# Gathering each tile of routed tokens by a slot-to-token table, in place of a scatter into a cleared buffer

## The chip, the cores and the metric

One core of a Trainium2 chip runs the kernel. The metric is the device time of one execution in microseconds (us). PE is TensorE, DVE is VectorE, ACT is ScalarE, POOL is GpSimd and SP is SyncE; SP and POOL issue the DMA transfers here.

## The reference

Four residual blocks run over x of shape (4, 512, 512), that is 2,048 tokens of 512 numbers, each behind a layer norm: a matmul with fp8-rounded operands, a mixture-of-experts FFN, cross attention with 16 heads, and a gated FFN with a Hadamard transform. Only the second matters here:

```python
xt = x.reshape(B * S, H)
sh_mid = gelu(einsum('th,ehd->ted', xt, Wsh_up))          # 2 shared experts, D = 256
shared_out = einsum('ted,edh->th', sh_mid, Wsh_down)
probs = softmax(xt @ W_router)                            # 16 routed experts
top_v, top_i = top_k(probs, 2)
gate = sum(one_hot(top_i, 16) * top_v[..., None], axis=1)
rt_mid = gelu(einsum('th,ehd->ted', xt, Wrt_up))
routed_out = einsum('ted,edh->th', rt_mid * gate[:, :, None], Wrt_down)
```

## The kernel before

The kernel runs phase by phase. `experts_phase` does the FFN with experts, from about 135 to 490 us of the span. Every float32 product is made in three passes from operands split into a high part (by ACT, `*_hi`) and a rest (by DVE, `*_lo`).

**Routing.** DVE writes the normalised tokens to `xn` (16 tiles of 128 tokens), PE transposes them (`turn_all`) and multiplies them by the router's weights (`route`). DVE then picks two experts for each token (`choose`). PE counts, by products with a triangle and with ones, how many tokens ahead of each one chose the same expert (`place_tokens`). From that DVE works out a slot for each token and choice, `slot[0]` and `slot[1]`, and the expert of each tile of 128 slots, `tile_expert`. Each expert's slots begin on a tile of their own, so there are up to NSLOT = 47 tiles.

**Dense part.** Eight units (four batches of 512 tokens, two shared experts) run on PE as `up(s)` and `down(s)`: `up` gives two banks, ACT puts the gelu on them and splits them, DVE makes the rest (`low(s)`), `down` gives four tiles, and DVE adds each to `x_res` (`add(s)`). `down` has three banks in turn, so that its tile n waits for the addition of tile n - 3. For batches 2 and 3 the transposed tokens are made again in the midst of the units (`turn_again` on PE, `again_hi` on ACT, `again_lo` on DVE). On each engine the order is written out by hand; PE's is up(0), up(1), place_tokens, down(0), up(2), turn_again(2), up(3), a wait for again_lo(2), down(1), down(2), turn_again(3), up(4), and so on. DVE's is assign_places, assign_slots(0), add(0), assign_slots(1), assign_tiles, low(2), again_lo(2), add(1), low(3), add(2), again_lo(3), and so on.

**The way of the tokens.** POOL sets a row of zeros, SP writes it over all of the DRAM tensor `tokens_by_expert` (47 tiles, `cleared`), and then POOL scatters each tile of `xn` to the slots of its first and of its second choice, 32 indirect DMAs (`scattered`). SP has one queue in order: for tile i it loads the expert's up weights and down weights (512 KB each, ring of four), then tile i of the tokens into `xg` (256 KB, ring of three, and for i = 0 only when all scatters have landed), then it stores the output of tile i - 6.

**Routed stage.** For each of the 47 tiles PE transposes `xg` (`turn(n)`, line 1153), multiplies by the up weights, transposes the gelu'd middle and multiplies by the down weights; ACT and DVE split all operands, ACT writes the output `y_out`. The attention phase then gathers the two outputs of each token from DRAM by `slot` with indirect DMAs on POOL (lines 1448 and 1455).

Of the kernel before, what the change touches and what calls it, by code (L numbers as in the profile page):

```python
# [5 lines left out]
F32 = mybir.dt.float32  # L6
F32R = mybir.dt.float32r
BF16 = mybir.dt.bfloat16
U32 = mybir.dt.uint32
# [553 lines left out]
def experts_phase(nc, Wsh_up, Wsh_down, Wrt_up, Wrt_down, W_router, x_res, ident, stats, head_weights,  # L563
# [4 lines left out]

    xg_dram = nc.dram_tensor("tokens_by_expert", (NSLOT * P, D), F32, kind="Internal").ap()
    with ExitStack() as ctx:  # L572
        al = Alloc(nc, ctx, "e")
        up_raw = al.sb("up_raw", [2, KD, DE])
# [3 lines left out]
        down_hi = al.sb("down_hi", [2, KE, D], F32R)  # L578
        down_lo = al.sb("down_lo", [2, KE, D], F32R)
        router_raw = al.sb("router_raw", [KD, E_RT])  # L580
        zeros = al.sb("zeros", [KD])
        probs = al.sb("probs", [NT, E_RT])
        rest = al.sb("rest", [NT, E_RT])
        first = al.sb("first", [NT, E_RT])
# [14 lines left out]
        passed = al.sb("passed", [NSLOT, E_RT])  # L599
        tile_f = al.sb("tile_f", [NSLOT])  # L600
        tile_expert = al.sb("tile_expert", [NSLOT], I32)
        xn = al.sb("xn", [NT, D])
        xg = al.sb("xg", [XG_RING, D])
        bank = [al.ps(f"bank{i}", [S]) for i in range(8)]
# [1 line left out]
        down_bank = bank[4:7]  # L606
        aux = bank[7]
        turn_bank = bank[0:7]
        logits_bank = aux[:, 0:NT * E_RT].rearrange("p (t e) -> p t e", e=E_RT)
        place_bank = aux[:, 0:(NT + 1) * E_RT].rearrange("p (t e) -> p t e", e=E_RT)  # L610
        xgT_bank, mid_bank = bank[0:2], bank[2:4]
# [34 lines left out]
        gate_chain = al.sem("gate_chain")  # L646
        shifted = al.sem("shifted")
        const_ready = al.sem("const_ready")
        zeros_ready = al.sem("zeros_ready")
        cleared = al.sem("cleared")  # L650
        chosen_ready = al.sem("chosen_ready")
        placed = al.sem("placed")
        slots_ready = al.sem("slots_ready")
        map_ready = al.sem("map_ready")
        scattered = al.sem("scattered")
        up_done = al.sem("up_done")
        gelu_ready = al.sem("gelu_ready")
        mid_hi_ready = al.sem("mid_hi_ready")
# [19 lines left out]
        @block.sync  # L678
        def _(sp):
            sp.dma_start(router_raw[:, :, :], rows(W_router)).then_inc(router_in, 16)  # L680
            for i in range(E_SH):
                sp.dma_start(up_raw[:, i], rows(Wsh_up[i])).then_inc(up_in[i], 16)
                sp.dma_start(down_raw[:, i], rows(Wsh_down[i])).then_inc(down_in[i], 16)
            sp.wait_ge(zeros_ready, 2)
            sp.dma_start(xg_dram.rearrange("(t p) d -> p t d", p=P),
                         xg[:, 0:1, :].to_broadcast([P, NSLOT, D])).then_inc(cleared, 16)

            up_flat = Wrt_up.rearrange("e (k p) m -> e p k m", p=P)
            down_flat = Wrt_down.rearrange("e (k p) m -> e p k m", p=P)

            def load(i):
                r = i % RAW_RING
                expert = sp.value_load(tile_expert[0:1, i:i + 1], min_val=0, max_val=E_RT - 1)
                if i < E_SH:
                    sp.wait_ge(up_ready, i + 1)
                elif i < RAW_RING:
                    sp.wait_ge(up_done, UNITS * KE)
                else:
                    sp.wait_ge(up_ready, E_SH + i - RAW_RING + 1)
                sp.dma_start(up_raws[r], up_flat[bass.ds(expert, 1)]).then_inc(up_in[r], 16)  # L700
                if i < E_SH:
                    sp.wait_ge(down_ready, i + 1)
                elif i >= RAW_RING:
                    sp.wait_ge(down_ready, E_SH + i - RAW_RING + 1)
                sp.dma_start(down_raws[r], down_flat[bass.ds(expert, 1)]).then_inc(down_in[r], 16)
                if i >= XG_RING:
                    sp.wait_ge(xg_turned, i - XG_RING + 1)
                if i == 0:
                    sp.wait_ge(scattered, 16 * 2 * NT)
                sp.dma_start(xg[:, i % XG_RING, :], xg_dram[i * P:(i + 1) * P, :]).then_inc(xg_in[i % XG_RING], 16)  # L710

            def store(i):
                sp.wait_ge(y_ready, i + 1)
                sp.dma_start(y_dram[i * P:(i + 1) * P, :], y_out[:, i % Y_RING, :]).then_inc(y_stored[i % Y_RING], 16)

            sp.wait_ge(map_ready, 1)
            for i in range(NSLOT):
                load(i)
                if i >= STORE_LAG:
                    store(i - STORE_LAG)  # L720
            for i in range(NSLOT - STORE_LAG, NSLOT):
                store(i)
            for i in range(Y_RING):
                sp.wait_ge(y_stored[i], 16 * len(range(i, NSLOT, Y_RING)))

        @block.gpsimd
        def _(pool):
            nc.clear_and_free_semaphores(retired)
            pool.memset(zeros[:, :], 0.0).then_inc(zeros_ready, 1)
            pool.memset(xg[:, 0, :], 0.0).then_inc(zeros_ready, 1)  # L730
            pool.wait_ge(zeros_ready, 1)
            for e in range(E_RT):
                pool.memset(rank[:, :, e:e + 1], float(E_RT - e)).then_inc(const_ready, 1)
            pool.memset(ones[:, :], 1.0).then_inc(const_ready, 1)
            pool.memset(chosen[:, NT, :], 0.0).then_inc(const_ready, 1)
            for i in range(2):
                pool.memset(run[i][:, 0:8], 0.0).then_inc(const_ready, 1)
            pool.iota(tile_no[:, :], [[1, NSLOT]], base=0, channel_multiplier=0,
                      allow_small_or_imprecise_dtypes=True).then_inc(const_ready, 1)
            pool.wait_ge(const_ready, E_RT + 5)  # L740
            pool.affine_select(below[:, :], ones[:, :], [[1, P]], ALU.is_gt, 0.0, base=0,
                               channel_multiplier=-1).then_inc(const_ready, 1)

            for name in "qkvo":
                head_weights.load(pool, name, 0)
            pool.wait_ge(cleared, 16)
            for i in range(2):
                pool.wait_ge(slots_ready, i + 1)
                for j in range(NT):
                    pool.indirect_dma_start(  # L750
                        xg_dram[:, :], bass.IndirectOffsetOnAxis(ap=slot[i][:, j:j + 1], axis=0), xn[:, j, :], None,
                        bounds_check=NSLOT * P - 1, oob_is_err=False).then_inc(scattered, 16)
        @block.scalar
        def _(act):
            def unit(s):
# [124 lines left out]
        def _(dve):  # L880
# [35 lines left out]
            def choose():  # L916
                dve.wait_ge(exp_ready, 1)
                link(dve.tensor_reduce(top[:, :], probs[:, :, :], AX.X, ALU.add))
                link(dve.reciprocal(inv[:, :], top[:, :]))
                link(dve.tensor_tensor(probs[:, :, :], probs[:, :, :], wide(inv), ALU.mult))  # L920
                dve.wait_ge(const_ready, E_RT + 6)
                pick(probs[:, :, :], first[:, :, :], gate[0])
                link(dve.scalar_tensor_tensor(out=rest[:, :, :], in0=first[:, :, :], scalar=-2.0, in1=probs[:, :, :],
                                              op0=ALU.mult, op1=ALU.add))
                pick(rest[:, :, :], rest[:, :, :], gate[1])
                dve.tensor_tensor(chosen[:, 0:NT, :], first[:, :, :], rest[:, :, :], ALU.add).then_inc(chosen_ready, 1)
# [21 lines left out]
            def assign_tiles():  # L948
                link(dve.tensor_tensor(passed[0:1], tile_no[0:1, :].unsqueeze(2).to_broadcast([1, NSLOT, E_RT]),
                                       run[0][0:1, 8:].unsqueeze(1).to_broadcast([1, NSLOT, E_RT]), ALU.is_ge))  # L950
                link(dve.tensor_reduce(tile_f[0:1, :], passed[0:1], AX.X, ALU.add))
                dve.tensor_scalar(tile_expert[0:1, :], tile_f[0:1, :], float(E_RT - 1), None,
                                  ALU.min).then_inc(map_ready, 1)

            def norm(b):
                for i in range(TB * b, TB * (b + 1)):
# [41 lines left out]
            assign_tiles()  # L998
            low(2)
            again_lo(2)  # L1000
            add(1)
            low(3)
            add(2)
            again_lo(3)
            low(4)
            add(3)
# [40 lines left out]

        @block.tensor
        def _(pe):
            def turn_all(b):  # L1050
                for j in range(TB):
                    n = TB * b + j
                    pe.wait_ge(xn_ready, n + 1)
                    if n >= 7:
                        pe.wait_ge(x32_ready, n - 6)
                    for k in range(KD):
                        ins = pe.transpose(turn_bank[n % 7][:, k * P:(k + 1) * P], xn[:, n, k * P:(k + 1) * P], ident[:, :])
                    ins.then_inc(x32_turned, 1)
# [71 lines left out]
            up(3)  # L1130
            pe.wait_ge(again_ready, TB)
            down(1)
            down(2)
            turn_again(3)
            up(4)
            pe.wait_ge(again_ready, 2 * TB)
# [31 lines left out]
            def turn_mid(n):  # L1168
                pe.wait_ge(gmid_ready, n + 1)
                if n == 0:  # L1170
                    pe.wait_ge(slots_ready, 2)
                elif n == 1:
                    pe.wait_ge(added, UNITS * TB)
                else:
# [978 lines left out]
```

## Time and profile before

| | |
|---|---|
| median of 3 runs | 2151.6 us (2144.74 to 2157.84) |
| the profiled execution | 2148.4 us, its span 2146.8 us |
| PE busy | 2007.4 us, 94% of the span |
| DVE busy | 1318.8 us, 61% |
| ACT busy | 842.2 us, 39% |
| POOL busy | 863.7 us, 40% |
| mean of TensorE's granted clock | 0.978 of full speed |

The span runs from the first to the last instruction of one profiled execution. A share of busy time is a mean over stages; what a change in one stage is worth has to be read in that stage. In a timeline a row gives the start, the length, the engine and line, and in brackets how long the engine had stood idle before and what ended it. "issue" is a wait that the profile can't put down to anything, "remote" an event from outside the engines.

### The profile page before, as it was taken

How to read it: one execution, taken by the hardware profiler on the slowest of the kernel's cores; microseconds unless marked ns; L12 is line 12 of the kernel's file. 1: busy time of each engine (PE TensorE's matmuls, PEld its weight loads, DVE VectorE, ACT ScalarE, POOL GpSimd, SP SyncE). 2: the span in 40 equal slices, each digit the busy share in tenths (PEclk: the TensorE clock that was granted, in tenths of full speed). 3: DMA queues.
4: the chain of work that ended last, by engine and by line, in shares of the span. 5: the costliest groups of instructions: out<-in, count | busy, mean ns of one | idle time of the engine just before them, and what ended most of it. 6: DMA issues, size and time to landing. Idle time of an engine off the chain costs nothing. (4 is left out here: it accounts for less than half of the span.)

```text
span 2146.8 us, 29048 instructions
## 1 busy us (share of the span) xinstructions
PE 2007.4 (94%) x9845; PEld 1663.7 (77%) x9849; DVE 1318.8 (61%) x2072; ACT 842.2 (39%) x1639; POOL 863.7 (40%) x739
## 2 busy tenths in 40 slices
PE   4987799994899999999999999999989999999999
PEld 4776577773778888888788888888867888888887
DVE  8975368887677766768676566666675333333333
ACT  4532158882434444445444444444432111111111
POOL 1104100003677766666766657665551222202200
PEclk9988899997999999999999999999999999999999
DMA  8366259994566656566555555555530011001002
GB/s 287 121 235 257 74 187 388 394 352 149 177 187 187 181 170 186 164 187 182 167 152 159 166 156 156 154 161 165 158 113 30 30 30 30 20 10 29 0 1 78
DMA packets 170320, 323.70 MB, mean 151 GB/s; under 512 B 16113, under 2 KB 41585, under 8 KB 170225
## 3 DMA queue, kind: packets, MB, share of 16 engines
q1 hardware_dynamic: 155120, 272.12, 40.8%
q0 software_dynamic: 15104, 50.34, 7.2%
q8 instruction: 55, 0.90, 0.2%
q14 instruction: 41, 0.33, 0.0%
HBM read 210.73 MB, written 111.67 MB: 150 GB/s over the span
## 5 line engine op out<-in xcount | busy, mean ns | idle before, releaser
L1393 POOL TENSOR_TENSOR t_pT_lo<-t_pT_raw,t_pT_hi 128x512 fp32r<-128x512 f32 x256 | 328.3, 1302 | 215.2 <-ACT t_pT_hi L1509 213.5
L1617 DVE TENSOR_REDUCE t_sums<-t_score 128x1 f32<-128x512 f32 x256 | 169.5, 688 | 130.3 <-PE t_score L52 129.9
L1991 DVE TENSOR_TENSOR f_lin<-f_lin,f_silu 128x512 f32<-128x512 f32 x64 | 44.8, 700 | 290.6 <-PE f_lin L52 290.6
L1524 ACT ACTIVATE t_probs<-t_score,t_sums 128x512 f32<-128x512 f32 x256 | 175.0, 684 | 84.3 <-DVE t_sums L1617 69.0
L1607 DVE STREAM_TRANSPOSE t_blocks<-t_probs 128x512 f32<-128x512 f32 x256 | 172.6, 693 | 20.4 <-ACT t_probs L1524 20.1
L1599 DVE SCALAR_TENSOR_TENSOR x_res<-t_out,t_sums,x_res 128x512 f32<-128x512 f32 x256 | 179.4, 741 | 4.7 <-PE t_out L52 4.5
L1509 ACT ACTIVATE t_pT_hi<-t_pT_raw 128x512 fp32r<-128x512 f32 x256 | 159.9, 625 | 1.1 <-DMA t_pT_raw<-turned_blocks 1.1
L1952 ACT ACTIVATE f_silu<-f_gate 128x512 f32<-128x512 f32 x64 | 38.3, 598 | 299.1 <-PE f_gate L52 299.1
L1503 ACT ACTIVATE t_o_hi<-t_o 128x512 fp32r<-128x512 f32 x64 | 38.3, 598 | 218.0 <-PE t_o L52 218.0
L1489 ACT ACTIVATE t_k_hi<-t_score 128x512 fp32r<-128x512 f32 x64 | 38.3, 598 | 204.6 <-PE t_score L52 200.9
L52 PE MATMUL t_score<-t_wv_hi,t_cT_hi 128*128 128x256 f32 x416 | 117.9, 283 | 0.7 <-ACT t_probs L1524 0.7
L52 PE MATMUL t_score<-t_wv_lo,t_cT_hi 128*128 128x256 f32 x416 | 117.9, 283 | 0.0
L52 PE MATMUL t_score<-t_wv_hi,t_cT_lo 128*128 128x256 f32 x416 | 117.8, 283 | 0.0
L52 PE MATMUL t_out<-t_wo_hi,t_o_hi 128*128 128x512 f32 x256 | 105.0, 410 | 12.8 <-DVE t_o_lo L1592 8.1
L2012 DVE TENSOR_TENSOR x_res<-f_down,x_res 128x512 f32<-128x512 f32 x128 | 88.1, 689 | 44.1 <-PE f_down L52 44.1
L52 PE MATMUL t_score<-t_k_hi,t_q_hi 128*128 128x512 f32 x256 | 102.8, 402 | 12.8 <-DVE t_v_lo L1586 4.8
L1582 DVE TENSOR_TENSOR t_k_lo<-t_score,t_k_hi 128x512 fp32r<-128x512 f32 x64 | 44.3, 691 | 113.2 <-ACT t_k_hi L1489 109.2
L52 PE MATMUL t_score<-t_cT_hi,t_wk_hi 128*128 128x512 f32 x256 | 101.5, 397 | 12.2 <-DVE t_cT_lo L1681 12.2
L1455 POOL DMA_INDIRECT t_blocks<-outputs_by_expert,slot x4 | 4.6, 1143 | 268.9 <-POOLq L572 267.9
L52 PE MATMUL t_q<-t_xT_hi,t_wq_hi 128*128 128x512 f32 x256 | 100.5, 393 | 2.8 <-DVE t_xT_lo L234 2.8
L52 PE MATMUL t_score<-t_k_lo,t_q_hi 128*128 128x512 f32 x256 | 101.3, 396 | 0.0
L52 PE MATMUL t_out<-t_wo_lo,t_o_hi 128*128 128x512 f32 x256 | 101.3, 396 | 0.0
(325 smaller groups left out, 6004.3 us busy)
## 6 DMA issues: line engine op xcount, KB each, us to landing
turned_blocks<-t_blocks SPq DMA_DIRECT2D x256, 256.0 KB
t_pT_raw<-turned_blocks SPq DMA_DIRECT2D x256, 256.0 KB, 4.1
e_up_raw<-in_L_ffn_Wrt_up_dram SPq DMA_DIRECT2D x47, 512.0 KB, 6.4
e_down_raw<-in_L_ffn_Wrt_down_dram SPq DMA_DIRECT2D x47, 512.0 KB, 5.9
tokens_by_expert<-e_xg SPq DMA_DIRECT2D x1, 12032.0 KB, 41.4
e_xg<-tokens_by_expert SPq DMA_DIRECT2D x47, 256.0 KB, 6.1
outputs_by_expert<-e_y_out SPq DMA_DIRECT2D x47, 256.0 KB, 6.2
wq_raw<-in_L_xattn_Wq_dram POOLq DMA_DIRECT2D x32, 256.0 KB, 4.6
```

The lines of the kernel that those rows point to most:

```text
L52: ins = pe.matmul(out, w(k), x(k), start=(k == 0 and j == 0), stop=(k == k_tiles - 1 and j == 2))
L1393: pool.tensor_tensor(pT_lo[:, q], pT_raw[:, q], f32(pT_hi[:, q]), ALU.subtract).then_inc(p_ready, 1)
L1489: act.activation(k_hi[:, :], score_bank[0][:, :], ACT.Copy).then_inc(k_hi_ready, 1)
L1503: act.activation(o_hi[:, :].rearrange("p (u q j) -> p q u j", q=Q4, j=BLK), o_bank[:, :].rearrange("p (q u j) -> p q u j", q=Q4, j=BLK), A ...
L1509: act.activation(pT_hi[:, q], pT_raw[:, q], ACT.Copy).then_inc(p_hi_ready, 1)
L1524: act.activation(probs[:, t % 2, :], score_bank[t][:, :], ACT.Exp, bias=neg_max[:, t:t + 1], accum_out=inv[:, p, t:t + 1]).then_inc(exp_re ...
L1582: dve.tensor_tensor(k_lo[:, :], score_bank[0][:, :], f32(k_hi[:, :]), ALU.subtract).then_inc(k_ready, 1)
L1599: dve.scalar_tensor_tensor(out=x_tile, in0=out_bank[t % 2][:, :], scalar=inv[:, p, t:t + 1], in1=x_tile, op0=ALU.mult, op1=ALU.add).then_i ...
L1607: dve.transpose(blocks[:, :, :, t, :].rearrange("p a t j -> p t a j"), probs[:, t % 2, :].rearrange("p (t a j) -> p t a j", a=Q4, j=BLK)). ...
L1617: dve.tensor_reduce(neg_max[:, t:t + 1], score_bank[t][:, :], AX.X, ALU.max, negate=True).then_inc(max_ready, 1)
L1991: dve.tensor_tensor(lin_bank[k][:, :], lin_bank[k][:, :], silu[:, k, :], ALU.mult).then_inc(mid_done, 1)
L2012: dve.tensor_tensor(x_tile, down_bank[t][:, :], x_tile, ALU.add).then_inc(added, 1)
```

## The change

The place of the routed tokens in DRAM, its clearing and the scatters go. In their stead SP stores `xn` as it is to DRAM (`normalised_tokens`, four transfers of 1 MB, each when its batch is normalised). A table is made that says for each slot which token is in it: a slot is split into its place in a tile (low seven bits) and its tile. DVE makes two one-hots, `at_place` (128 places for each of 16 token tiles) and `at_tile` (47 tiles, once weighted by the token's row and once by its tile number), in `mark(i)` for choice i. PE multiplies them, 16 products of 94 columns for each choice, all into one bank (`find_tokens(i)`), and DVE puts row and tile number together (`number_tokens`). POOL then gathers tile n of the tokens by column n of that table, straight from DRAM into `xg`. Empty slots have token 0. SP's loop is left with the weights and the stores. The new steps stand at fixed places of the orders written by hand.

```diff
@@ SP
-            sp.wait_ge(zeros_ready, 2)
-            sp.dma_start(xg_dram.rearrange("(t p) d -> p t d", p=P),
-                         xg[:, 0:1, :].to_broadcast([P, NSLOT, D])).then_inc(cleared, 16)
+            for b in range(B):
+                sp.wait_ge(xn_ready, TB * (b + 1))
+                sp.dma_start(xn_dram[b * S:(b + 1) * S, :].rearrange("(t p) d -> p t d", p=P),
+                             xn[:, TB * b:TB * (b + 1), :]).then_inc(xn_stored, 16)
...
-                if i >= XG_RING:
-                    sp.wait_ge(xg_turned, i - XG_RING + 1)
-                if i == 0:
-                    sp.wait_ge(scattered, 16 * 2 * NT)
-                sp.dma_start(xg[:, i % XG_RING, :], xg_dram[i * P:(i + 1) * P, :]).then_inc(xg_in[i % XG_RING], 16)
@@ POOL
-            pool.memset(zeros[:, :], 0.0).then_inc(zeros_ready, 1)
-            pool.memset(xg[:, 0, :], 0.0).then_inc(zeros_ready, 1)
-            pool.wait_ge(zeros_ready, 1)
...
-            pool.wait_ge(cleared, 16)
-            for i in range(2):
-                pool.wait_ge(slots_ready, i + 1)
-                for j in range(NT):
-                    pool.indirect_dma_start(
-                        xg_dram[:, :], bass.IndirectOffsetOnAxis(ap=slot[i][:, j:j + 1], axis=0), xn[:, j, :], None,
-                        bounds_check=NSLOT * P - 1, oob_is_err=False).then_inc(scattered, 16)
+            pool.wait_ge(xn_stored, 16 * B)
+            pool.wait_ge(tokens_ready, 1)
+            for n in range(NSLOT):
+                if n >= XG_RING:
+                    pool.wait_ge(xg_turned, n - XG_RING + 1)
+                pool.indirect_dma_start(
+                    xg[:, n % XG_RING, :], None, xn_dram[:, :], bass.IndirectOffsetOnAxis(ap=token[:, n:n + 1], axis=0),
+                    bounds_check=NT * P - 1, oob_is_err=False).then_inc(xg_in[n % XG_RING], 16)
@@ DVE
+            def mark(i):
+                if i == 1:
+                    dve.wait_ge(token_found, 1)
+                link(dve.tensor_scalar(place_u[:, :], slot[i][:, :], P - 1, None, ALU.bitwise_and))
+                link(dve.tensor_scalar(tile_u[:, :], slot[i][:, :], 7, None, ALU.logical_shift_right))
+                link(dve.tensor_copy(place_of[:, :], place_u[:, :]))
+                link(dve.tensor_copy(tile_of[:, :], tile_u[:, :]))
+                each = lambda a, n: a.unsqueeze(1).to_broadcast([P, NT, n])
+                of = lambda a, n: a.unsqueeze(2).to_broadcast([P, NT, n])
+                link(dve.tensor_tensor(at_place[:, :, :], each(place_no[:, :], P), of(place_of[:, :], P), ALU.is_equal))
+                link(dve.tensor_tensor(at_tile[:, :, 0, :], each(tile_no[:, :], NSLOT), of(tile_of[:, :], NSLOT),
+                                       ALU.is_equal))
+                link(dve.tensor_tensor(at_tile[:, :, 1, :], at_tile[:, :, 0, :], of(tile_count[:, :], NSLOT), ALU.mult))
+                dve.tensor_scalar(at_tile[:, :, 0, :], at_tile[:, :, 0, :], row_no[:, 0:1], None,
+                                  ALU.mult).then_inc(marked, 1)
+
+            def number_tokens():
+                dve.wait_ge(token_found, 2)
+                link(dve.tensor_copy(tile_f[:, :], token_bank[:, 0:NSLOT]))
+                dve.scalar_tensor_tensor(out=token[:, :], in0=token_bank[:, NSLOT:2 * NSLOT], scalar=float(P),
+                                         in1=tile_f[:, :], op0=ALU.mult, op1=ALU.add).then_inc(tokens_ready, 1)
...
             again_lo(2)
+            mark(0)
             add(1)
             low(3)
+            mark(1)
             add(2)
+            number_tokens()
             again_lo(3)
@@ PE
+            def find_tokens(i):
+                pe.wait_ge(marked, i + 1)
+                for j in range(NT):
+                    ins = pe.matmul(token_bank, at_place[:, j, :], at_tile[:, j, :, :].rearrange("p a n -> p (a n)"),
+                                    start=(i == 0 and j == 0), stop=(i == 1 and j == NT - 1))
+                ins.then_inc(token_found, 1)
...
             down(1)
+            find_tokens(0)
             down(2)
+            find_tokens(1)
             turn_again(3)
...
                 if n == 0:
-                    pe.wait_ge(slots_ready, 2)
+                    pe.wait_ge(tokens_ready, 1)
```

Three short `iota` instructions on POOL (the numbers 0 to 127, the row, and 0 to 15) take the place of its two `memset`s.

## Rows read from the trace of the kernel before

**Rows 1.** Windows: us, PE, PEld, DVE, ACT, POOL busy, PEclk, DMA share, GB/s.

```profile
150.00:160.00 10.00, 10.00 (x69) 10.00 (x69) 0.00 (x0) 4.28 (x6) 0.00 (x0) 0.72 1.05 410
200.00:230.00 30.00, 9.09 (x18) 5.24 (x18) 1.72 (x3) 1.65 (x3) 19.14 (x20) 0.59 0.49 191
260.00:270.00 10.00, 10.00 (x45) 8.05 (x44) 3.36 (x5) 1.98 (x4) 0.00 (x0) 1.00 0.00 1
500.00:508.00 8.00, 8.00 (x33) 6.84 (x34) 5.63 (x8) 0.60 (x1) 6.17 (x7) 0.62 0.92 319
320.00:400.00 80.00, 75.20 (x478) 62.19 (x477) 69.04 (x81) 70.26 (x120) 0.00 (x0) 1.00 1.06 390
```

**Rows 2.** Instructions of line 750, the scatters: ns least/median/most, first and last start.

```profile
L750 POOL DMA_INDIRECT tokens_by_expert<-e_xn,slot x32: 976/976/1106, 184.0 to 223.9; - x32
```

**Rows 3.** Timeline of ACT beside the scatters.

```profile
206.27 0.60 ACT L783 ACTIVATE e_xT_hi<-e_bank 128x512 fp32r<-128x512 f32 x1 [5.75 <-remote]
229.46 0.58 ACT L759 ACTIVATE e_bank<-e_bank 128x512 f32<-128x512 f32 x1 [22.59 <-remote]
```

**Rows 4.** Timeline of PE, 177 to 242.

```profile
177.56 1.12 PE L1111 MATMUL e_bank<-e_chosen,e_ones 128*128 128x256 bf16 x16
...
193.76 0.66 PE L1077 MATMUL e_bank<-ident,e_xn 128*128 128x128 f32 x4 [1.31 <-DVE e_xT_lo L968]
...
199.60 0.40 PE L52 MATMUL e_bank<-e_xT_hi,e_up_lo 128*128 128x512 f32 x1
207.65 0.79 PE L52 MATMUL e_bank<-e_down_hi,e_mid_hi 128*128 128x512 f32 x1 [7.65 <-issue]
...
214.00 0.39 PE L52 MATMUL e_bank<-e_down_lo,e_mid_hi 128*128 128x512 f32 x1 [1.50 <-issue]
...
239.75 0.39 PE L52 MATMUL e_bank<-e_down_lo,e_mid_hi 128*128 128x512 f32 x1
239.98 0.40 PE L52 MATMUL e_bank<-e_down_hi,e_mid_lo 128*128 128x512 f32 x1
241.16 1.53 PE L1077 MATMUL e_bank<-ident,e_xn 128*128 128x128 f32 x12 [0.79 <-DVE x_res L902]
```

**Rows 5.** Instructions of line 1153, the transpositions of the 47 routed tiles.

```profile
L1153 PE MATMUL e_bank<-ident,e_xg x188: 270/273/331, 294.2 to 477.4; 128*128 128x128 f32 x188
```

**Rows 6.** Waits, 320 to 470: us in all, times, longest.

```profile
PEld e_bank L1153 <- DMA e_xg<-tokens_by_expert: 25.2, 37, 1.3
ACT e_y_out L861 <- DMA outputs_by_expert<-e_y_out: 20.1, 38, 1.7
```

**Rows 7.** DMA issues of the page, the clearing: KB, us to landing.

```profile
tokens_by_expert<-e_xg SPq DMA_DIRECT2D x1, 12032.0 KB, 41.4
```

**Rows 8.** Timeline of DVE, operations of the sizes that the change adds.

```profile
167.39 2.29 DVE L962 TENSOR_TENSOR e_xT_lo<-e_x,e_xT_hi 128x2048 fp32r<-128x2048 f32 x1
...
180.51 0.81 DVE L936 TENSOR_TENSOR e_run<-e_run 128x16 f32<-128x16 f32 x4
...
187.29 0.93 DVE L949 TENSOR_TENSOR e_passed<-e_tile_no,e_run 1x752 f32<-1x752 f32 x1
```

**Rows 9.** Timelines of POOL, ACT and PE beside eight gathers.

```profile
543.67 1.07 POOL L1448 DMA_INDIRECT ffn_raw<-outputs_by_expert,slot  x1 [25.10 <-DVE t_cT_lo L1681]
...
550.28 0.39 PE L52 MATMUL t_score<-t_cT_hi,t_wk_lo 128*128 128x512 f32 x1
...
552.36 0.60 ACT L1489 ACTIVATE t_k_hi<-t_score 128x512 fp32r<-128x512 f32 x1 [3.73 <-remote]
...
553.78 0.69 PE L52 MATMUL t_score<-t_k_hi,t_q_hi 128*128 128x512 f32 x1 [3.11 <-issue]
554.26 0.63 PE L52 MATMUL t_score<-t_k_lo,t_q_hi 128*128 128x512 f32 x1
```

**Rows 10.** Instructions of line 1455, gathers of the outputs, and their landing.

```profile
L1455 POOL DMA_INDIRECT t_pT_raw<-outputs_by_expert,slot x4: 1014/1271/1653, 494.7 to 503.8; - x4
...
DMA to landing us min/median/max: 4.1/4.7/5.3
```

More of the change, by code:

```diff
@@ L564, in experts_phase @@
                   y_dram, gate, slot, retired):
-    xg_dram = nc.dram_tensor("tokens_by_expert", (NSLOT * P, D), F32, kind="Internal").ap()
+    xn_dram = nc.dram_tensor("normalised_tokens", (NT * P, D), F32, kind="Internal").ap()
     with ExitStack() as ctx:
@@ L580, in experts_phase @@
         router_raw = al.sb("router_raw", [KD, E_RT])
-        zeros = al.sb("zeros", [KD])
         probs = al.sb("probs", [NT, E_RT])
@@ L601, in experts_phase @@
         tile_expert = al.sb("tile_expert", [NSLOT], I32)
+        place_no, row_no, tile_count = al.sb("place_no", [P]), al.sb("row_no", [1]), al.sb("tile_count", [NT])
+        place_u, tile_u = al.sb("place_u", [NT], U32), al.sb("tile_u", [NT], U32)
+        place_of, tile_of = al.sb("place_of", [NT]), al.sb("tile_of", [NT])
+        at_place = al.sb("at_place", [NT, P], BF16)
+        at_tile = al.sb("at_tile", [NT, 2, NSLOT], BF16)
+        token = al.sb("token", [NSLOT], U32)
         xn = al.sb("xn", [NT, D])
@@ L608, in experts_phase @@
         turn_bank = bank[0:7]
+        token_bank = aux[:, (NT + 1) * E_RT:(NT + 1) * E_RT + 2 * NSLOT]
         logits_bank = aux[:, 0:NT * E_RT].rearrange("p (t e) -> p t e", e=E_RT)
@@ L648, in experts_phase @@
         const_ready = al.sem("const_ready")
-        zeros_ready = al.sem("zeros_ready")
-        cleared = al.sem("cleared")
+        xn_stored = al.sem("xn_stored")
+        marked, token_found, tokens_ready = al.sem("marked"), al.sem("token_found"), al.sem("tokens_ready")
         chosen_ready = al.sem("chosen_ready")
@@ L654, in experts_phase @@
         map_ready = al.sem("map_ready")
-        scattered = al.sem("scattered")
         up_done = al.sem("up_done")
@@ L739, in _ @@
                       allow_small_or_imprecise_dtypes=True).then_inc(const_ready, 1)
-            pool.wait_ge(const_ready, E_RT + 5)
+            pool.iota(place_no[:, :], [[1, P]], base=0, channel_multiplier=0,
+                      allow_small_or_imprecise_dtypes=True).then_inc(const_ready, 1)
+            pool.iota(row_no[:, :], [[1, 1]], base=0, channel_multiplier=1,
+                      allow_small_or_imprecise_dtypes=True).then_inc(const_ready, 1)
+            pool.iota(tile_count[:, :], [[1, NT]], base=0, channel_multiplier=0,
+                      allow_small_or_imprecise_dtypes=True).then_inc(const_ready, 1)
+            pool.wait_ge(const_ready, E_RT + 8)
             pool.affine_select(below[:, :], ones[:, :], [[1, P]], ALU.is_gt, 0.0, base=0,
@@ L920, in choose @@
                 link(dve.tensor_tensor(probs[:, :, :], probs[:, :, :], wide(inv), ALU.mult))
-                dve.wait_ge(const_ready, E_RT + 6)
+                dve.wait_ge(const_ready, E_RT + 9)
                 pick(probs[:, :, :], first[:, :, :], gate[0])
```

## The prediction

> **What bounds the kernel now.** I read the page first. TensorE (PE) is busy for 94% of the span, as the table above says, so what a change is worth depends on the few places where PE stands still. I then cut the experts phase into windows and looked for a low PE figure. The dense part has PE at 10.00 us of 10, but from 200 to 230 PE is busy for 9.09 us of 30, and DVE and ACT for 1.7 us each [rows 1]. The DMA engines moved 191 GB/s there, where the clearing transfer reached 410. So all engines wait, and not for bandwidth.
>
> The instructions of POOL and the timelines of ACT and PE say more. POOL issues the 32 scatters from 184.0 to 223.9, one every 1.29 us [rows 2]. ACT splits its last transposed tile at 206.27, though PE had started that transposition at 193.76 and ended it by 194.4, and then does nothing for 22.59 us [rows 3, 4]. PE waits for this chain until 207.65. Then come matmuls inside one product, which wait for no semaphore, and one of them stands behind 1.50 us of "issue" [rows 4]. The pace is normal again soon after the last scatter. I read this as: while scatters are in flight, the sequencers hand out instructions very slowly. How that comes about no row shows.
>
> In the routed stage each of the 47 tiles takes (477.4 - 294.2) / 46 = 3.98 us [rows 5]. The DMA share is 1.06 at 390 GB/s; over 150 us and some 37 tiles PE's weight loads wait 25.2 us for `e_xg` and ACT 20.1 us for the stores [rows 1, 6]. That is a loop near the limit of the DMA engines, with ACT and DVE busy for 70.26 and 69.04 us of 80.
>
> **The change, part by part.**
>
> *Clearing and scatter out.* The clearing (12,032 KB, 41.4 us to land [rows 7]) lies under work of PE that needs none of it, so it is worth nothing by itself. The four 1 MB stores of `xn` in its place are a third of the bytes and hidden in the same stretch. With the scatters goes, if I read it rightly, the stall. What is that worth? up(3) ends at 199.85. down(1) and down(2) are 24 matmuls each at 0.23 us (the spacing of the two before turn_again) = 5.6 us each, then comes the 0.8 us wait for add(2): turn_again(3) could start at 199.85 + 11.2 + 0.8 = 211.85. It started at 241.16 [rows 4]. **Gross: -29.3 us.**
>
> *mark(0) and mark(1) on DVE, find_tokens on PE.* A mark has four operations on 16 elements at 0.2 us (0.84 with their gaps), one on 2,048 elements, as `e_xT_lo` (2.29), three on 752, as `e_passed` (2.79), and four gaps of 0.04: 6.1 us [rows 8]. Place decides what shows of it, so I went through both orders. again_lo(2) ends at 195.7 (0.6 us on PE, ACT and DVE each behind 193.76). mark(0) runs 195.7 to 201.8. down(1) runs 199.85 to 205.45 and its tiles are added from 202.7 to 206.2: no wait. find_tokens(0) is 16 short bf16 products; the 16 of place_tokens, 136 columns wide in the mean against 94, took 1.12 us [rows 4]: until 206.55. mid_hi(3) needs down(1)'s end, its second half comes at 207.4, low(3) ends at 208.1, and mark(1), behind it, at 214.2. Behind mark(1) stands add(2). down(2) does three tiles until 210.75; its fourth needs add(2)'s first addition, 214.2 + 0.7 = 214.9. **That is a new stall of PE of 4.1 us.** The fourth tile ends at 216.3, find_tokens(1) at 217.4, and it covers the old 0.8 us wait. turn_again(3) starts at 217.4, so the additions cost 217.4 - 211.85 = 5.6 us. Bounds: 2.2 us (the products alone, marks hidden) and 14.4 us (marks and products fully exposed).
>
> *Clock.* After an idle of 3.11 us PE came back at the lower of its two levels, 1.2 GHz: matmuls of 0.69 and 0.63 us where 0.39 is usual, for some 3 us, eight matmuls each 0.2 us late = 1.6 us [rows 9]. I add 1.6 for the new stall (bounds 0 and 3.2): turn_again(3) at 219.0. **So far: 219.0 - 241.16 = -22.2 us.** All that follows in the dense part hangs on a PE at 10 of 10 us and moves up with it. number_tokens is two small operations beside transpositions.
>
> *Gathers.* 47 indirect gathers on POOL replace 47 plain loads on SP. The first three are issued near 219, some 50 us before they are needed. A later one waits for turn(n - 3), so it has 3 x 3.98 = 12 us; gathers took 1.0 to 1.65 us on POOL and landed 4.1 to 5.3 us behind their issue [rows 10]: on time. Bytes stay 1.5 MiB a tile. On SP's queue each load and store has one transfer fewer ahead, so the waits for `e_xg` and for stores shrink, but by the DMA engines at most 183 x (1 - 390/410) = 8.9 us can be had. Against that stands that gathers disturb engines too: eight were issued from 543.67 on, and beside them ACT took `t_k_hi` at 552.36, though PE had ended its input at 550.7; 1.7 us late, 0.21 us a gather [rows 9]. Over 47 tiles that is 10 us if nothing absorbs it, but ACT has 20.1 / 37 = 0.5 us of idle a tile. I take 0 for the loop, with -8.9 and +10 as ends.
>
> The Trainium skill, "SBUF — State Buffer", section "SBUF: two separate sides", speaks against this part: GpSimd and a VectorE operation in a two-port mode exclude each other for the whole instruction, so that descriptors of a GpSimd DMA can't be written meanwhile. The trace agrees at most in part: one gather took 1.65 us where most of its neighbours took 1.0. By the rule alone the time would be that of the second rival, 2151; by the row it is the sum below.
>
> **Sum.** -29.3 + 5.6 + 1.6 + 0 = -22.2 us by the clock times above. The profiled execution took 2148.4 us (span 2146.8), the median of the runs is 2151.6: profiling adds nothing that can be seen, so the stall belongs to the ordinary run as well. 2151.6 - 22.2 = **2129.4 us**. A difference under 0.5%, 10.8 us, can hardly be told from none.
>
> **The rivals.**
>
> 1. *Each gather holds up the sequencers.* In the scatters' stall single instructions lost 1.50 us [rows 4]. If each gather costs the loop half of one such hold, 0.75 us, the stage gains 47 x 0.75 = 35 us: 2151.6 - 22.2 + 35 = 2164, slower. It turns the sign from 22.2 / 47 = 0.47 us a tile. For it: [rows 9] show a delay of 0.21 us a gather. Against it: from 500 to 508, in the midst of sixteen gathers, PE was busy for 8.00 us of 8 [rows 1], and one gather in 4 us is a third of that density. 9%.
> 2. *Gathers wait for DVE.* DVE is busy 69.04 / 80 x 3.98 = 3.43 us a tile [rows 1]. If a gather of 1.0 us fits only beside that, the period is 4.43 us, +0.45 x 47 = +21: 2151, no change. Against it: the longest gather beside DVE's work took 1.65 us [rows 10]. 8%.
> 3. *The stall isn't the scatters'.* Something else holds the engines from 200 to 229 and stays; the marks vanish in it and only the products, 2.2 us, are added: 2154, no change. Against it: the stall begins some 10 us behind the first scatter and ends with them. 7%. By the skill's same section transfers and engines have separate ports, so scatters shouldn't slow an engine; no row shows ports.
> 4. *The loop gains as well.* With `xg` off SP's queue the period falls to the DMA engines' limit: 2129.4 - 8.9 = 2120.5. 18%.
>
> My own case, the loop within 5 us of today's, has 58%.
>
> **How the numbers follow.** Faster by over 0.5% (below 2140.8): my case and rival 4, less 0.02 for costs near their upper bounds, 0.74. Within 0.5%: rivals 2 and 3 and that rest, 0.18 with a little of rival 1. Slower: the rest of rival 1, 0.08. The range starts at 2117, rival 4 with marks of 4 instead of 6.1 us; it reaches to 2150, which is where the upper bounds together lead (-29.3 + 14.4 + 3.2 + 10 = -1.7), and leaves out half of the no-change cases and the slower one. The likeliest case alone: 2122 to 2137.
>
> **What would show it.** Windows behind 195 have PE at 9 to 10 of 10 us but for one idle of about 4 us ahead of the fourth tile of down(2), ended by DVE's `x_res`. Each mark is 6 us of DVE. PE's first transposition of `e_xg` starts near 272 instead of 294.2. From there on a tile takes 3.9 to 4.1 us, with one gather each on POOL, and PE's wait for `e_xg` falls or moves to the weights. I am wrong if "issue" or "remote" idles stand on PE and ACT all through the routed stage (rival 1), if gathers last 2 us and more and PE waits for them (rival 2), or if the stall near 200 is still there (rival 3).

## The result, and the profile after

The changed kernel took 2133.42 us in the median of 4 runs (2123.97 to 2140.55), the kernel before 2152.72 us (2144.74 to 2157.84). The ratio on record is 0.9901 with a 95% interval of 0.9874 to 0.9928, so the gain lies between 15.5 and 27.1 us: faster, by about 1%. The two medians by themselves differ by 19.3 us. The profiled execution took 2140.55 us (span 2138.9), which is at the slow end of its four runs. Why it is there matters for reading it, so I begin with the stages, worked out as differences of start times in the two timelines of PE:

| stretch | before | after | difference |
|---|---|---|---|
| first transposition of `xn` to up(0) | 28.14 | 37.75 | +9.6 |
| up(0) to turn_again(3) | 77.04 | 53.81 | -23.2 |
| turn_again(3) to the first transposition of `e_xg` | 53.0 | 52.8 | -0.2 |
| first to last transposition of `e_xg` | 183.2 | 189.0 | +5.8 |
| from there to the first product of attention | 22.5 | 20.7 | -1.7 |
| attention and FFN | 1646.8 | 1647.7 | +0.9 |

With 1.0 us that the phase began later this makes -7.8, the difference of the spans (-7.9) but for rounding. Windows of the changed kernel (columns as in [rows 1]):

```profile
150.00:160.00 10.00, 10.00 (x50) 10.00 (x49) 0.61 (x1) 2.26 (x5) 0.00 (x0) 0.50 0.86 335
160.00:180.00 20.00, 20.00 (x83) 18.87 (x82) 5.01 (x5) 7.92 (x9) 0.00 (x0) 0.50 0.00 1
200.00:230.00 30.00, 25.03 (x140) 19.88 (x139) 21.56 (x36) 6.53 (x13) 0.00 (x0) 0.94 0.22 71
```

Between 200 and 230 PE is busy for 25.03 us where it was 9.09 [rows 1]: the stall is gone. But from 150 to 180 the granted clock is at the lower level, 1.2 GHz, where the window of before showed 0.72. PE does the same routing work without a pause in both, so it takes longer. It isn't part of the change, as the experiments show: the same kernel has either length. What decides between them no run shows. Now the place where the prediction had put a new wait, first on PE and then on DVE:

```profile
216.06 0.87 PE L1087 MATMUL e_bank<-e_at_tile,e_at_place 128*128 128x94 bf16 x16
...
224.86 0.79 PE L52 MATMUL e_bank<-e_down_hi,e_mid_hi 128*128 128x512 f32 x1 [3.66 <-DVE x_res L910]
225.45 0.63 PE L52 MATMUL e_bank<-e_down_lo,e_mid_hi 128*128 128x512 f32 x1
...
227.59 1.09 PE L1087 MATMUL e_bank<-e_at_tile,e_at_place 128*128 128x94 bf16 x16
228.57 1.53 PE L1118 MATMUL e_bank<-ident,e_xn 128*128 128x128 f32 x12
```

```profile
219.50 2.29 DVE L973 TENSOR_TENSOR e_at_place<-e_place_no,e_place_of 128x2048 bf16<-128x2048 f32 x1
221.83 0.94 DVE L974 TENSOR_TENSOR e_at_tile<-e_tile_no,e_tile_of 128x752 bf16<-128x752 f32 x1
222.81 0.94 DVE L976 TENSOR_TENSOR e_at_tile<-e_at_tile,e_tile_count 128x752 bf16<-128x752 bf16 x1
223.78 0.42 DVE L977 TENSOR_SCALAR e_at_tile<-e_at_tile,e_row_no 128x752 bf16<-128x752 bf16 x1
224.12 1.88 DVE L910 TENSOR_TENSOR x_res<-e_bank,x_res 128x512 f32<-128x512 f32 x3
```

The addition at 224.12 comes behind mark(1), PE's fourth tile of down(2) behind that addition, after 3.66 us of idle, and its six matmuls run at the lower clock (0.79 and 0.63 us). In the routed stage (transpositions, gathers with ns least/median/most, and waits from 320 to 470; they answer to [rows 5, 6]):

```profile
L1196 PE MATMUL e_bank<-ident,e_xg x188: 270/272/417, 281.4 to 470.4; 128*128 128x128 f32 x188
```

```profile
L757 POOL DMA_INDIRECT e_xg<-normalised_tokens,e_token x47: 997/1300/1518, 230.1 to 456.6; - x47
```

```profile
POOL e_xg L757 <- PE e_bank L1196: 96.9, 34, 3.7
ACT e_y_out L869 <- DMA outputs_by_expert<-e_y_out: 23.0, 33, 2.8
...
PEld e_bank L52 <- issue: 13.3, 31, 2.5
```

No row has PE waiting for `e_xg` any more, and POOL waits for PE instead, 2.8 us each time. ACT still waits for the stores, 23.0 us in 33 waits where it was 20.1 in 38 [rows 6].

### The profile page after: what moved, and what is told of

Its sections match the earlier page's. It is cut to its first block and busy times, and to the rows that moved or that the text cites. A ratio compares the mean times of both kernels' runs of the same rounds, so it can differ in the third digit from the quotient of the medians.

```text
span 2138.9 us, 29117 instructions
## 1 busy us (share of the span) xinstructions
PE 2019.6 (94%) x9877; PEld 1675.9 (78%) x9881; DVE 1329.2 (62%) x2090; ACT 843.0 (39%) x1639; POOL 890.9 (42%) x755
## 5 line engine op out<-in xcount | busy, mean ns | idle before, releaser
L757 POOL DMA_INDIRECT e_xg<-normalised_tokens,e_token x47 | 59.7, 1270 | 256.1 <-PE e_bank L1196 167.2
L52 PE MATMUL t_out<-t_wo_hi,t_o_lo 128*128 128x512 f32 x256 | 102.5, 400 | 0.0
```

The costliest lines, as they stand in the source:

```text
L52: ins = pe.matmul(out, w(k), x(k), start=(k == 0 and j == 0), stop=(k == k_tiles - 1 and j == 2))
L757: pool.indirect_dma_start(xg[:, n % XG_RING, :], None, xn_dram[:, :], bass.IndirectOffsetOnAxis(ap=token[:, n:n + 1], axis=0), bounds_chec ...
```

## The experiments

All times are medians of the runs. The ratio is to the kernel before, run beside on the same chip; where there is none, the kernel ran once. e1, e8, e9, e3 and e4 leave routed tokens out or fetch others; they are tests, and their time is no offer.

| kernel | us | ratio, 95% interval | first transposition to up(0) | up(0) to turn_again(3) | routed stage |
|---|---|---|---|---|---|
| before | 2152.72 | | 28.14 | 77.04 | 183.2 |
| after | 2133.42 | 0.9901 (0.9874 to 0.9928) | 37.75 | 53.81 | 189.0 |
| e12, after again | 2127.52 | one run | 28.36 | 52.69 | 186.6 |
| e1, no scatters | 2129.0 | 0.9874 (0.9836 to 0.9911) | 37.53 | 48.06 | 188.5 |
| e8, 16 scatters | 2134.3 | 0.9905 (0.9877 to 0.9932) | 28.15 | 52.19 | 181.8 |
| e9, 32 gathers instead | 2160.82 | one run | 37.55 | 76.45 | 184.6 |
| e10, scatters held apart | 2129.07 | one run | 37.54 | 47.91 | 181.5 |
| e2, clearing back | 2133.71 | 0.9891 (0.9844 to 0.9937) | 37.62 | 54.07 | 185.3 |
| e3, plain loads | 2137.3 | 0.9918 (0.9889 to 0.9947) | 37.75 | 53.87 | 186.2 |
| e4, rows in order | 2128.44 | 0.9883 (0.9843 to 0.9923) | 28.35 | 53.73 | 181.5 |
| e5, mark(1) later | 2130.8 | 0.9884 (0.9857 to 0.9911) | 28.36 | 48.49 | 187.8 |
| e6, empty slots skipped | 2119.75 | 0.9843 (0.9812 to 0.9873) | 32.28 | 53.36 | 179.1 |
| e7, e5 and e6 | 2116.74 | 0.9821 (0.9795 to 0.9846) | 29.06 | 48.49 | 178.1 |
| e11, e7 and four outputs | 2113.62 | 0.9819 (0.9790 to 0.9849) | 38.45 | 48.50 | 173.2 |

The last three columns come from each kernel's one profile. The first of them is near 28 or near 38 (32 once) whatever the kernel, so it is to be left out when kernels are compared.

### Is it the scatters? (e1, e8)

```diff
# e1, on the kernel before
-            for i in range(2):
-                pool.wait_ge(slots_ready, i + 1)
-                for j in range(NT):
-                    pool.indirect_dma_start(xg_dram[:, :], ..., xn[:, j, :], ...).then_inc(scattered, 16)
...
-                    sp.wait_ge(scattered, 16 * 2 * NT)
+                    sp.wait_ge(cleared, 16)
# e8, on the kernel before
-            for i in range(2):
+            for i in range(1):
...
-                    sp.wait_ge(scattered, 16 * 2 * NT)
+                    sp.wait_ge(scattered, 16 * NT)
```

> The kernel before, with its 32 scatters left out; SP's first load of a token tile waits for the clearing instead, so that all routed tiles are zeros and the routed output is wrong. If the scatters cause the stall of 200 to 230 us (my theory), PE has no idle 'issue' rows there, turn_again(3) starts about 47 to 48 us behind up(0) instead of 77.0, and the time is 29 us below the kernel before, near 2123. If something else holds the engines there (rival: fetching of instructions, or what the early part of the dense stage does by itself), the 77 us and the time stay.

> The kernel before with the 16 scatters of the first choice alone; half of the routed tokens are left zero, so the output is wrong. The scatters last 20.6 us instead of 41.3. If the engines are held whenever scatters are in flight, the stall lasts half as long or less: the loss against no scatters falls from 29 to between 5 and 12 us (it began some 10 us behind the first scatter). If the loss doesn't depend on the number of scatters, it stays at 29.

Without scatters the dense stretch takes 48.06 us instead of 77.04: the 32 scatters cost 29.0 us. With 16 of them it takes 52.19: 4.1 us, less than the 5 to 12 expected. The cost isn't proportional: the second half of the scatters does 25 of the 29 us.

### Scatters, or any indirect transfers of POOL, and in what manner? (e9, e10)

```diff
# e9, on the kernel before: 32 gathers at the scatters' place, eight buffers
                 for j in range(NT):
+                    n = NT * i + j
+                    if n >= 8:
+                        pool.wait_ge(burst[n % 8], 16 * (n // 8))
                     pool.indirect_dma_start(
-                        xg_dram[:, :], ..., xn[:, j, :], ...).then_inc(scattered, 16)
+                        spare[:, n % 8, :], None, xg_dram[:, :],
+                        bass.IndirectOffsetOnAxis(ap=slot[i][:, j:j + 1], axis=0),
+                        bounds_check=NSLOT * P - 1, oob_is_err=False).then_inc(burst[n % 8], 16)
# e10, on the kernel before
                 for j in range(NT):
+                    if NT * i + j >= 2:
+                        pool.wait_ge(scattered[j % 2], 16 * ((NT * i + j) // 2))
                     pool.indirect_dma_start(
...
```

> The kernel before with each of its 32 scatters replaced at its place by a gather of the same number of rows, from the cleared DRAM tensor by the same indices into eight spare buffers (at most eight in flight); the routed tokens are left zero, so the output is wrong. Is it the scatter or any burst of indirect transfers from POOL that holds the engines? If only scatters do (writes to DRAM), turn_again(3) starts 48 to 50 us behind up(0), as without scatters. If any burst does, it starts at about 77, as before.

> The kernel before with its 32 scatters held apart: POOL issues one only when the last but one has landed, so two are in flight at most; the output is the reference's. If the engines are held because scatters pile up (many in flight), they are held little or not at all: turn_again(3) starts 48 to 55 us behind up(0) instead of 77.0, though the scatters last longer. If each scatter in flight holds them, the loss is as long as the scatters last, and it starts at 77 or later.

With 32 gathers the stretch takes 76.45 us, as with the scatters. Timeline of PE, beside POOL's row for those gathers:

```profile
220.78 0.58 PE L52 MATMUL e_bank<-e_down_hi,e_mid_lo 128*128 128x512 f32 x1 [2.10 <-issue]
241.40 0.80 PE L52 MATMUL e_bank<-e_down_hi,e_mid_hi 128*128 128x512 f32 x1 [20.04 <-DVE x_res L908]
```

```profile
L755 POOL DMA_INDIRECT e_spare<-tokens_by_expert,slot x32: 997/1002/1122, 195.0 to 235.7; - x32
```

The first gather starts at 195.0, the last at 235.7, one every 1.31 us without a pause, and PE is free again when they end. Held apart, the same 32 scatters of the kernel before cost nothing: 47.91 us. POOL and the window:

```profile
228.66 0.97 POOL L753 DMA_INDIRECT tokens_by_expert<-e_xn,slot  x1 [1.65 <-DMA tokens_by_expert<-e_xn,slot]
229.94 0.97 POOL L753 DMA_INDIRECT tokens_by_expert<-e_xn,slot  x1 [0.30 <-issue]
232.12 0.97 POOL L753 DMA_INDIRECT tokens_by_expert<-e_xn,slot  x1 [1.20 <-DMA tokens_by_expert<-e_xn,slot]
```

```profile
200.00:230.00 30.00, 27.31 (x133) 22.08 (x132) 13.43 (x21) 8.87 (x16) 15.39 (x17) 1.00 0.46 175
```

The DMA engines moved 175 GB/s there, nearly what they moved in the stall (191), and PE was busy for 27.31 us of 30. So it isn't enough that scatters are in flight, nor is it their bytes; and with e9, it isn't that they write to DRAM. What holds the engines is a long row of indirect transfers that POOL works off without a pause.

Is it that more of them are in flight without e10's waits? The traces let them be counted, since each transfer is 80 packets of the software queue (2,560 for the 32). DMA of the kernel before, from 184 to 215 and from 184 to 224:

```profile
q0 software_dynamic: 1840, 6.03, 48.1%
tokens_by_expert<-e_xn,slot POOLq DMA_INDIRECT x25
```

```profile
q0 software_dynamic: 2400, 7.87, 48.5%
tokens_by_expert<-e_xn,slot POOLq DMA_INDIRECT x32
```

At 215 the packets of 1840 / 80 = 23 transfers out of 25 had been moved, at 224 those of 30 out of 32. So in the midst of the stall two are in flight, no more than in e10, and their number isn't what holds the engines there. Nor do they wait for their instructions to be fetched: from 187.2 to 244.4 no packet runs on the queues q8 and q14, which carry instructions, and PE takes up its pace at 230.41 all the same. Two differences to e10 remain, which no run separates. POOL pauses 0.30 us between two transfers of the kernel before, and in e10 mostly 1.2 us behind every second one. And POOL's sequencer runs far ahead of POOL in the kernel before (its last `MOVE` for a scatter comes at 208.3, 15.6 us ahead of that scatter), in e10 by 1.0 us (249.9 and 250.9). How either reaches PE and ACT no row shows.

The one run of e10 is 2129.07 us with the long routing stretch: as far as one run can tell, a wait in POOL alone brings as much as the whole change.

### Is the clearing worth nothing? (e2, e12)

```diff
# e2, on the changed kernel
+            sp.wait_ge(zeros_ready, 1)
+            sp.dma_start(xg_dram.rearrange("(t p) d -> p t d", p=P),
+                         xg[:, 0:1, :].to_broadcast([P, NSLOT, D])).then_inc(cleared, 16)
             for b in range(B):
                 sp.wait_ge(xn_ready, TB * (b + 1))
```

> The changed kernel with the 12 MB clearing put back, from a row of zeros into a DRAM tensor that nobody reads. If the clearing was worth nothing, the time is that of the changed kernel within noise (2124 to 2141), and so is the length of each stage. A rival says that the clearing, by filling the DMA engines from 138 to 178, kept TensorE's granted clock up in routing: the changed kernel's profile has 34 us at the lower level there against 14 us before. Then this run has 14 us or less of it and is some 10 us faster than the changed kernel's profiled 2140.55. If the clock there is chance, it falls either way whatever the kernel.

> The changed kernel, unchanged, for a second profile. It tells what of two stages is the kernel's and what is chance. From the first transposition to up(0) it took 37.75 us in the profile after and 28.14 in that of before, with four of the other kernels near either length; it will be one of the two. The routed stage took 189.0 us; if that was mostly the steps of 5.00 and 7.39 us on the empty tiles, I expect steps of 4.4 us or more there again and a stage between 185 and 189.

With the clearing back the median is 2133.71 us and the ratio 0.9891, no difference from the changed kernel that could be seen. It has the long routing stretch all the same, so the clearing doesn't keep the clock up. The changed kernel itself has the short one in its second profile. That profile's windows:

```profile
150.00:160.00 10.00, 10.00 (x64) 10.00 (x63) 0.00 (x0) 4.29 (x6) 0.00 (x0) 0.67 0.67 258
160.00:180.00 20.00, 19.77 (x91) 16.44 (x92) 15.71 (x30) 9.18 (x12) 0.00 (x0) 0.82 0.00 0
```

Its one run took 2127.52, the profiled one of the first series 2140.55. Six profiles have 28.1 to 29.1 us, seven 37.5 to 38.5, one 32.3, in kernels with the same work there. So something that isn't in the kernel puts 9 to 10 us on an execution, nearly half of what this change is worth.

### What made the routed stage longer? (e3, e4, e6)

```diff
# e3, on the changed kernel: SP loads, at its old place
+                sp.dma_start(xg[:, i % XG_RING, :], xn_dram[(i % NT) * P:(i % NT + 1) * P, :]).then_inc(xg_in[i % XG_RING], 16)
# e4, on the changed kernel
+            pool.iota(in_order[:, :], [[0, 3], [P, NT]], base=0, channel_multiplier=1).then_inc(const_ready, 1)
-                    ... bass.IndirectOffsetOnAxis(ap=token[:, n:n + 1], axis=0)
+                    ... bass.IndirectOffsetOnAxis(ap=in_order[:, n:n + 1], axis=0)
# e6, on the changed kernel: a slot without a token gets 4096
-            pool.iota(tile_count[:, :], [[1, NT]], base=0, ...
+            pool.iota(tile_count[:, :], [[1, NT]], base=-2 * NT, ...
-                link(dve.tensor_copy(tile_f[:, :], token_bank[:, 0:NSLOT]))
+                link(dve.tensor_scalar(tile_f[:, :], token_bank[:, 0:NSLOT], float(2 * NT * P), None, ALU.add))
+            pool.memset(xg[:, :, :], 0.0).then_inc(const_ready, 1)
```

> The changed kernel with plain loads of 128 consecutive rows of the stored tokens, issued by SP at their old place in its queue, in place of the 47 gathers; the table is still made but not used, so the routed output is wrong. The routed stage (first to last transposition of a tile) took 183.2 us before and 189.0 after. If the gathers cost those 5.8 us, this run is back at 183 and its time 6 us below the changed kernel. If they come from something else in the change (the order of SP's queue, chance), it stays at 189.

> The changed kernel with its 47 gathers by POOL, but with indices that count up, so that each gather fetches 128 consecutive rows and no row twice; the routed output is wrong. It tells two causes of the slower routed stage apart. (a) What costs is that the last tiles have no tokens and fetch row 0 over and over: the last steps there took 5.00 and 7.39 us. Then this run has no such steps and its stage takes 183 to 184 us. (b) What costs is a gather by POOL as such, 0.1 us on each tile: then the stage stays near 187 to 189 and the extra time is spread over all tiles.

> The changed kernel in which a slot without a token gets an index above the bounds, so that the gather leaves it out (1,920 of 6,016 rows), instead of row 0; the output is the reference's. If the repeated row 0 costs the time at the end of the routed stage, the stage falls from 189.0 to about 183; and with 5% fewer bytes in a stage whose DMA share is over 1, up to 5 us more, to 178. If only a gather as such costs, the stage stays at 187 to 189.

Plain loads don't bring the stage back to 183 (186.2), gathers of rows in order do and more (181.5). So a gather as such costs nothing that can be seen, and the 0.21 us for each that I had as an upper bound was too dark. But the stage scatters by itself: five kernels that load plainly from the tensor of slots (before, e1, e8, e9, e10) have 181.5 to 188.5, mean 183.9; the four that gather row 0 for empty slots (after, e12, e2, e5) have 185.3 to 189.0, mean 187.2. The difference, 3.3 us, is no larger than what one profile can be off, so the 5.8 us of the first table are in good part chance. What is firm is the end. PE at the last tiles of the changed kernel:

```profile
450.20 0.60 PE L1196 MATMUL e_bank<-ident,e_xg 128*128 128x128 f32 x4
...
455.19 0.60 PE L1196 MATMUL e_bank<-ident,e_xg 128*128 128x128 f32 x4
460.02 0.62 PE L52 MATMUL e_bank<-e_down_hi,e_midT_hi 128*128 128x512 f32 x1 [2.33 <-issue]
462.58 1.05 PE L1196 MATMUL e_bank<-ident,e_xg 128*128 128x128 f32 x4
```

The step of 7.39 us was seen once: in e12 the last six steps are 4.08 to 4.45 us, shorter than I expected, while its stage of 186.6 us is as expected. But the mean of the last six steps from tile to tile is 4.29 to 4.77 us in the four kernels that gather row 0, and 3.99 to 4.12 in before, e1, e3, e4, e8, e9 and e10. The two groups don't meet: the repeated row costs 0.2 to 0.8 us a tile there, 1 to 5 us in all. Skipping the empty slots, 1,920 rows of 6,016, gives 179.1 and, in e7, 178.1 us, the lowest with three output buffers, and the interval of e6's ratio (0.9812 to 0.9873) lies just below that of the changed kernel. It removes both the repeated row and bytes, so how much is due to each stays open.

### Can the new stall be moved away, and do the gains add? (e5, e7, e11)

```diff
# e5, on the changed kernel: DVE, then PE
-            mark(1)
             add(2)
-            number_tokens()
             again_lo(3)
+            mark(1)
             low(4)
             add(3)
+            number_tokens()
...
-            find_tokens(1)
             turn_again(3)
             up(4)
+            find_tokens(1)
# e11, on e7
-XG_RING, Y_RING, RAW_RING, STORE_LAG = 3, 3, 4, 6
+XG_RING, Y_RING, RAW_RING, STORE_LAG = 3, 4, 4, 6
```

> The changed kernel with mark(1) behind again_lo(3) instead of ahead of add(2), find_tokens(1) behind up(4) instead of ahead of turn_again(3), and number_tokens behind add(3). If the place of mark(1) costs what the profile after shows (PE idle 3.66 us ahead of down(2)'s fourth tile, and 1.6 us of lower clock behind it), this run has neither and is 4 to 5.5 us faster than the changed kernel in the dense stage. Rival: the marks' 5.7 us of DVE are late wherever they stand, PE then waits in down(3) for add(3) or for low(4), and nothing is won.

> Both edits, the later mark(1) and the skipped empty slots. If they are independent, their gains add: 4 to 5.5 us in the dense stage and 6 to 11 in the routed one, so 10 to 16 us below the changed kernel, near 2120 in the median. If the second is hidden behind another wait, it is no better than the better one of the two alone.

> The kernel with the later mark(1) and the skipped empty slots, and four output buffers instead of three. In the routed stage ACT still waits for the store three tiles back to land (24.3 us in 36 tiles of the changed kernel). If that wait sets the pace, the stage falls from 178.1 us to 170 or less. If the DMA engines' rate does, ACT waits for something else and the stage stays at 176 to 179.

In e5 turn_again(3) comes 48.49 us behind up(0), 5.3 less than after. But find_tokens(1) now stands behind up(4) and waits there for mark(1):

```profile
213.46 1.53 PE L1118 MATMUL e_bank<-ident,e_xn 128*128 128x128 f32 x12 [0.79 <-DVE x_res L910]
...
223.11 0.87 PE L1087 MATMUL e_bank<-e_at_tile,e_at_place 128*128 128x94 bf16 x16 [1.35 <-DVE e_at_tile L977]
```

So 2.2 us are given back: the first transposition of `e_xg` comes 103.53 us behind up(0) instead of 106.66, a gain of 3.1 us, a little under the 4 to 5.5 expected. In the ratios, 0.9884 against 0.9901, it can't be told from none. e7 has both edits, the dense stretch of e5 (48.49 us) and the routed stage of e6 (178.1 and 179.1 us), so the two don't hide each other, and its interval lies wholly below that of the changed kernel. e11's stage is the shortest of all, 173.2 us, between the two values expected. ACT's wait for stores is about half of what it was in e7 (14.7 us in 24 waits from 310 to 440). Waits of e11 from 300 to 440:

```profile
ACT e_y_out L870 <- DMA outputs_by_expert<-e_y_out: 7.3, 18, 0.9
```

That the shorter wait gives the 4.9 us is likely, but not shown: stages of one group of kernels differ by up to 7 us from profile to profile. The ratio of e11 is that of e7 (0.9819 and 0.9821); its profile had the long routing stretch. The two can't be told apart by their times, but both beat both kernels: e11 took 2113.62 against 2133.42 and 2152.72 us.

## Why the prediction was right, point by point

**The number.** Forecast 2129.4 us, 22.2 below the kernel before; measured 2133.42 us, 19.3 below by the medians and 21 by the ratio. Part of this closeness is luck: the dense part brought 1 to 2 us more than forecast, and the routed stage, forecast at 0, took 3.4 to 5.8 us in the two profiles.

**The stall and its worth.** Forecast -29.3 us gross, measured 77.04 - 48.06 = 29.0 (e1). The time without the stall was forecast as 211.85 - 164.12 = 47.7 us behind up(0), measured 48.06.

**The reading of the stall** was right in that the scatters cause it (e1) and wrong in how. "While scatters are in flight, the sequencers hand out instructions very slowly": e10 has scatters in flight for 57 us and nothing is held. What counts is the unbroken row. And of the sixteen gathers in attention I said that PE ran undisturbed beside them; that fits e8, where a row of 16 (scatters) cost 4.1 us, and it says little of a long row: 32 cost 29 us, gathers as well as scatters. With the condition wrong, it was in part luck that the new gathers did no harm: the ring of three sets them 4 us apart, and nothing like the hold of e9 is seen among them. Scatters 1.8 us apart in the mean were harmless too (e10); gathers closer than 4 us in the routed stage no run tried.

**Marks and products.** Forecast 6.1 us a mark, measured 218.68 to 224.20, 5.5: the last operation, of bf16 on 752 elements with a scalar, took 0.42 instead of 0.93. Forecast 4.1 us of new idle ahead of down(2)'s fourth tile, measured 3.66, at the place and by the releaser named. The products took 0.87 and 1.09 against 1.1. The lower clock behind the idle came too. All additions together: forecast 5.6 + 1.6 = 7.2 us, measured 53.81 - 48.06 = 5.75, and 4.6 in e12.

**Net of the dense part.** Forecast -22.2, measured -23.2, in e12 77.04 - 52.69 = -24.4.

**The loop.** Forecast 0 with -8.9 and +10 as ends; the first profile says +5.8, the second +3.4, and only 1 to 5 us at its end can be put down to the change, to row 0. PE's wait for `e_xg` vanished as forecast, and another took its place. What I hadn't seen is what it costs that all empty slots fetch the same row.

**Clearing.** Forecast nothing, and no difference was seen (e2).

**The rivals.** Rival 1 (each gather holds the sequencers) has its mechanism, in e9, but not at this density: e4's stage of 181.5 us shows none. (Single matmuls in the stall lost up to 2.42 us, not 1.50 as I had read, so its price was set low.) Rival 2 (gathers wait for DVE): they took 1.30 us in the median where those alone took 1.00, and up to 1.52, and POOL stood idle 2.8 us a tile. So the rule of the Trainium skill, "SBUF — State Buffer", section "SBUF: two separate sides", agrees in kind at most, and it decides nothing here; that DVE's work is what lengthens them wasn't tested. Rival 3 (another cause of the stall) falls with e1. By the same section of the Trainium skill transfers and engines don't share ports. e10 agrees, since 175 GB/s, most of it scatters, held nobody. Rival 4 (the loop gains as well) didn't come with the change, but e6 and e11 were 4 and 10 us below the 183.2, by other means than an emptier queue.

**Where I couldn't know.** The forecast names the first transposition of `e_xg` near 272; it came at 281.4, because routing ran at 1.2 GHz. Counted from up(0) it came 23.4 us earlier.

## What to carry to other kernels

When all engines crawl with "issue" and "remote" beside DMA engines that are half idle, look at what POOL issues: a long unbroken row of indirect transfers is suspect, and the cheapest test is a wait that holds them apart (e10). Before rebuilding an algorithm around such a stall, try that wait; here it gave in one run what the rebuilding gave. Compare stages, counted from a common event, before comparing spans: one stage whose clock was low in the first profile, whatever the kernel, hid nearly half of this gain there. And slots that hold nothing are better given an index out of bounds than one row for all.

## What the runs showed of the hardware that wasn't expected

- 32 indirect transfers by POOL, one every 1.3 us without a pause, held PE and ACT for 29 us, as scatters (77.04 against 48.06 us) and as gathers (76.45). 16 in a row cost 4.1 us. Two in flight at most, one every 1.8 us in the mean ((250.9 - 194.0) / 31), cost nothing (47.91). In the midst of the stall two were in flight as well (23 of 25 landed at 215, 30 of 32 at 224), so it isn't their number.
- TensorE's granted clock in the routing stretch, with PE busy throughout and the same work, was at 1.2 GHz for longer in some executions than in others of the same kernel: a share of 0.50 from 150 to 180 in the first profile of the changed one, 0.67 and 0.82 in the second. The stretch took 37.75 and 28.36 us, a difference of 9.4.
- A gather of 128 rows took 1.30 us on POOL in the routed stage and 1.00 in a row by itself.
